# Single-buffered score banks and a fourth bank for the maxima, in the attention loop of a Mamba-2 and mixture-of-experts layer

## The reference, cut to what matters

```python
# b = 2, s = 2048, d = 256, 16 heads of 16
q, k, v = (src @ w).reshape(b, s, 16, 16).transpose(0, 2, 1, 3)   # for w in q_w, k_w, v_w
scores = einsum('bhqd,bhkd->bhqk', q, k) / sqrt(16)
scale = sigmoid(einsum('bhsd,hd->bhs', q, scale_w)) * 2.0
aw = softmax(scores * scale[..., None], axis=-1)
out = einsum('bhqk,bhkd->bhqd', aw, v)
```

## Time and profile before

| | us |
|---|---|
| runs: median (lowest to highest) | 2485.02 (2483.46 to 2487.04) |
| profiled execution: its span | 2487.7 |
| profiled execution: time outside its span | not given |
| TensorE busy | 2369.6 |
| VectorE busy | 2102.9 |
| ScalarE busy | 1796.4 |
| first to last maximum (L1682) | 720.5 to 2094.9 |
| first to last exponential (L1647) | 776.7 to 2137.4 |

### The profile page before, as it was taken

How to read it: one execution, slowest core, us unless ns; L and a number is a source line. 1 busy time by engine, 2 the same in 40 slices (tenths; PEclk the granted TensorE clock), 3 DMA queues, 4 the chain that set the end, 5 groups by cost and what they waited for, 6 DMA issues and landing times. The chain is left out here.

```text
span 2487.7 us, 45337 instructions
## 1 busy us (share of the span) xinstructions
PE 2369.6 (95%) x16331; PEld 1028.3 (41%) x16331; DVE 2102.9 (85%) x4156; ACT 1796.4 (72%) x2368; POOL 992.7 (40%) x1186
## 2 busy tenths in 40 slices
PE   7899999999689999999999999999999999996996
PEld 5566655655443223223222222223223222473663
DVE  6778788989689999999998999898899996283886
ACT  4888887777334887878787787787787878762664
POOL 1687878888741222211221221221211011255664
PEclk8999999999889999999999999999999999997998
DMA  3322233223240220304012030040040000125892
GB/s 110 112 88 90 85 92 105 89 99 96 67 137 14 37 43 7 59 14 65 14 31 35 14 59 7 14 65 2 14 65 2 2 2 24 52 83 204 297 304 101
DMA packets 105956, 174.09 MB, mean 70 GB/s; under 512 B 21218, under 2 KB 80658, under 8 KB 100596
## 3 DMA queue, kind: packets, MB, share of 16 engines
q1 hardware_dynamic: 98996, 156.08, 23.6%
q0 software_dynamic: 6016, 14.49, 1.7%
q10 hardware_dynamic: 720, 0.62, 0.1%
HBM read 145.21 MB, written 27.02 MB: 69 GB/s over the span
## 5 line engine op out<-in xcount | busy, mean ns | idle before, releaser
L1682 DVE TENSOR_REDUCE max_part<-round_psum 128x1 f32<-128x512 f32 x2048 | 1269.0, 683 | 101.8 <-PE round_psum L1591 96.8
L1647 ACT ACTIVATE p_exp<-score_psum 128x1024 f32<-128x1024 f32 x1024 | 993.3, 1022 | 213.7 <-PE score_psum L1576 209.3
L1591 PE MATMUL round_psum<-k_stack,q_stack 64*128 64x512 bf16 x2048 | 705.5, 384 | 10.7 <-DVE max_part L1682 6.5
L1567 PE MATMUL score_psum<-q_stack,k_stack 64*128 64x512 bf16 x2048 | 599.0, 379 | 0.9 <-ACT p_exp L1647 0.2
L1576 PE MATMUL score_psum<-q_stack,k_stack 35*128 35x512 bf16 x2048 | 594.6, 378 | 0.0
L1622 PE MATMUL pv_psum<-p_exp,values 128*17 128x512 f32 x4096 | 539.6, 598 | 0.0
L1591 PEld LDWEIGHTS round_psum<-k_stack,q_stack 64*128 64x128 bf16 x2048 | 189.4, 93 | 600.3 <-DVE max_part L1682 510.7
L672 PE MATMUL rot<-tokens_t,w_in 128*128 128x512 f32 x576 | 271.7, 603 | 0.2
L1576 PEld LDWEIGHTS score_psum<-q_stack,k_stack 35*128 35x128 bf16 x2048 | 188.9, 94 | 116.0 <-issue 0.5
L1729 POOL TENSOR_TENSOR rden<-pv_out,minus_one 128x16 f32<-128x16 f32 x31 | 90.0, 2903 | 332.4 <-ACT pv_out L1665 330.1
L1715 POOL CAST max_parts<-max_neg 128x16 bf16<-128x16 f32 x96 | 20.4, 212 | 365.8 <-DVE max_neg L1688 343.4
(11 more groups left out here) (300 smaller groups left out, 3472.9 us busy)
## 6 DMA issues: line engine op xcount, KB each, us to landing
cum_rows_in<-cum_rows SPq DMA_DIRECT2D x64, 512.0 KB, 3.8
expert_w<-in_expert_w SPq DMA_DIRECT2D x24, 1028.0 KB
tokens_t<-in_expert_w SPq DMA_DIRECT2D x15, 1028.0 KB
cum_pairs_in<-cum_rows SPq DMA_DIRECT2D x240, 64.0 KB, 2.8
qk_rows<-qk_parts SPq DMA_DIRECT2D x64, 192.0 KB, 3.1
q_stack<-qk_rows SPq DMA_DIRECT2D x84, 128.0 KB, 8.1
k_stack<-qk_rows SPq DMA_DIRECT2D x84, 128.0 KB, 9.1
token_rows<-tokens SPq DMA_DIRECT2D x12, 512.0 KB, 3.7
```

The source lines that it names most:

```text
L1567: nc.tensor.matmul(ebank[i // 2][:, i % 2, :], ks[rows, n % 2, plane, k * P:(k + 1) * P], qs[rows, n % 2, plane, q * BLK:(q + 1) * BLK], s ...
L1591: nc.tensor.matmul(bank[step][:, :], qs[rows, n % 2, plane, at:at + P], ks[rows, n % 2, plane, keys * BLK:(keys + 1) * BLK], start=True, s ...
L1647: nc.scalar.activation(pt[:, (k * 2 + pair) % 4, :, :], ebank[pair][:, :, :], ACT.Exp).then_inc(*exped.up(u, k, pair))
L1682: nc.vector.tensor_reduce(mx[:, c * HG + h, keys:keys + 1], bank[step][:, :], AX_X, ALU.max).then_inc(*maxed.up(u, k, i))
```

## The change

`round_psum` gets a fourth bank, and its users wait for the user four back. `score_psum` becomes three single banks. Scores take them in the order in which they begin (heads 1, 0, 3, 2 of each step), and each "main" waits until the exponential of the score three back has been taken. Each "rest" now raises `scored`, and ScalarE takes one head of 512 columns at a time. The stage before gets its fourth bank (half of `vbank`) from the ring, for which TensorE waits for that stage's last values (`first.v_stored`) ahead of its first maximum. The late values go around the three score banks.

```diff
-    ebank = [ps(f"score_psum{i}", [P, 2, BLK]) for i in range(2)]
+    ebank = [ps(f"score_psum{i}", [P, BLK]) for i in range(3)]
     pv = ps("pv_psum", [P, BLK])
-    rbank = [ps(f"round_psum{i}", [P, BLK]) for i in range(3)]
+    rbank = [ps(f"round_psum{i}", [P, BLK]) for i in range(4)]
...
-                                [ebank[0][:, i, :] for i in range(2)], [ebank[1][:, i, :] for i in range(2)], rbank[0:2])
+                                ebank[0:2], [ebank[2], rbank[3]], rbank[0:2])
...
-    bank = {u: rbank[i % 3] for i, u in enumerate(users)}
-    before = {u: users[i - 3] for i, u in enumerate(users) if i >= 3}
-
+    bank = {u: rbank[i % 4] for i, u in enumerate(users)}
+    before = {u: users[i - 4] for i, u in enumerate(users) if i >= 4}
+
+    scores = [(u, k, i) for u in range(NU) for k in range(KT) for i in (1, 0, 3, 2)]
+    score_bank = {score: ebank[i % 3] for i, score in enumerate(scores)}
+    score_before = {score: scores[i - 3] for i, score in enumerate(scores) if i >= 3}
...
-    scored = sems.events("scored", pairs)
-    exped = sems.events("exp_ready", pairs)
+    scored = sems.events("scored", scores)
+    exped = sems.events("exp_ready", scores)
...
-        return ebank[c // 2 % 2][:, c % 2, 0:D]
+        return ebank[c % 3][:, 0:D]
...
-                    stack_on_sync(nc, sp_, S, u, j, i, scored.at((u - 1) * SB - 1, KT - 1, 1) if u >= 2 else None)
-
-            sp_.wait_ge(*scored.at(NU - SB - 1, KT - 1, 1))
+                    stack_on_sync(nc, sp_, S, u, j, i, scored.at((u - 1) * SB - 1, KT - 1, 2) if u >= 2 else None)
+
+            sp_.wait_ge(*scored.at(NU - SB - 1, KT - 1, 2))
...
+            pe.wait_ge(*first.v_stored)
             for step in order:
...
-                    if i % 2 and (u, k) != (0, 0):
-                        pe.wait_ge(*exped.at(*back(u, k, 1), i // 2))
+                    if (u, k, i) in score_before:
+                        pe.wait_ge(*exped.at(*score_before[u, k, i]))
...
-                    nc.tensor.matmul(ebank[i // 2][:, i % 2, :], ks[rows, n % 2, plane, k * P:(k + 1) * P],
+                    nc.tensor.matmul(score_bank[u, k, i][:, :], ks[rows, n % 2, plane, k * P:(k + 1) * P],
...
-                    if i % 2 == 0:
-                        m.then_inc(*scored.up(u, k, i // 2))
+                    nc.tensor.matmul(score_bank[u, k, i][:, :], ks[rows, n % 2, plane, k * P:(k + 1) * P],
+                                     qs[rows, n % 2, plane, q * BLK:(q + 1) * BLK], start=False,
+                                     stop=True).then_inc(*scored.up(u, k, i))
...
-                        pe.wait_ge(*first.v_stored)
-                    if c - 4 in late:
-                        pe.wait_ge(*v_stored.at(c - 4))
+                    if c - 3 in late:
+                        pe.wait_ge(*v_stored.at(c - 3))
...
-                            pe.wait_ge(*exped.at(u, k, h // 2))
+                            pe.wait_ge(*exped.at(u, k, h))
...
-                if what == "rest" and i % 2 == 0:
+                if what == "rest":
                     pair = i // 2
-                    act.wait_ge(*scored.at(u, k, pair))
-                    if (u, k) >= (0, 2):
+                    act.wait_ge(*scored.at(u, k, i))
+                    if i % 2 and (u, k) >= (0, 2):
                         act.wait_ge(*weighed.at(*back(u, k, 2), pair))
-                    nc.scalar.activation(pt[:, (k * 2 + pair) % 4, :, :], ebank[pair][:, :, :],
-                                         ACT.Exp).then_inc(*exped.up(u, k, pair))
+                    nc.scalar.activation(pt[:, (k * 2 + pair) % 4, i % 2, :], score_bank[u, k, i][:, :],
+                                         ACT.Exp).then_inc(*exped.up(u, k, i))
```

More of the change, by code:

```diff
@@ L1575, in _ @@
                             pe.wait_ge(*S.filled.all())
-                    m = nc.tensor.matmul(ebank[i // 2][:, i % 2, :], ks[rows, n % 2, plane, k * P:(k + 1) * P],
-                                         qs[rows, n % 2, plane, q * BLK:(q + 1) * BLK], start=False, stop=True)
-                    if i % 2 == 0:
-                        m.then_inc(*scored.up(u, k, i // 2))
+                    nc.tensor.matmul(score_bank[u, k, i][:, :], ks[rows, n % 2, plane, k * P:(k + 1) * P],
+                                     qs[rows, n % 2, plane, q * BLK:(q + 1) * BLK], start=False,
+                                     stop=True).then_inc(*scored.up(u, k, i))
                 if what == "max":
```

## The result

The changed kernel takes 2664.65 us (median of four runs, 2660.55 to 2665.32), the kernel before 2485.06 on the same chip: a ratio of 1.072, 95% interval 1.0704 to 1.0735, 180 us more. The forecast was 2668.

A forecast was written before the change was run, and what follows sets the result against it. VectorE's maxima (2.48 a step) were taken as the bound, nearly tied with TensorE. A same-step wait makes 511 periods of 2.83: 1446 + 24 + 71 = 1541, +182, with entry +184; span 2671, forecast 2668, range 2635 to 2702.

The forecast's parts named there:

- Head 2's "main" behind head 1's exponential: Attention step: head 2's first score matmul waits for head 1's exponential of the same step until 1.31; period 2.83, not 2.47.
- Sum over the attention: Attention loop: 511 periods of 2.83 (1446), 24 for turns and 71 for group insertions: 1541 us in place of 1359.8.
- ScalarE is not the bound: Attention step: four 512-column exponentials occupy ScalarE for 2.0 to 2.1 us against 1.94, which by throughput still fits into 2.47.
- Entry: Before the first maximum: TensorE waits for all value copies of the stage before, 1.8 us later, straight on the path.
- Total: Whole kernel: +184 us makes the profiled span 2671; less 2.7 for span against median, the forecast is 2668.
- Who set the step before: Old attention step: VectorE's four maxima at 0.620 fill the 2.48 period, nearly tied with TensorE's 2.39 to 2.40.
- rival A: Attention loop: same-step wait covered, fourth maxima bank saves up to 0.62 at each of 39 insertions, 24 us, 2461; chance 4%.
- The ring of four: Maxima's banks: removes the 0.08 wait at the sixth matmul pair, already counted, and gives nothing more in a plain step.
- Clock: Attention loop: TensorE keeps granted clock 1.00 despite longer pauses; the rival of a lost fast clock, 2790, had chance 5%.

## Why the prediction was right, and where it was not

- **Head 2's "main" behind head 1's exponential.** Right in each link: 0.65, 0.60, then "main" at 1.30 (1.31 forecast), the value matmuls at 1.84 (1.85), the period 2.82 to 2.83 (2.83), and 2.81 in the last unit, where 2.83 was forecast. The halved exponentials show that this chain carries the step, and that ScalarE's load does not.
- **Sum over the attention.** 1537.3 measured, 1541 forecast; the plain step of 2.82 and not 2.83 makes up the difference. An output's turn adds 0.59 (forecast 0.58), the rows' turn 0.21 (0.21), a projection 1.92 (1.92), a pair of casts 0.26 (0.27), a scale 1.01 (1.07).
- **ScalarE is not the bound.** Right: four exponentials in 2.17, 0.65 idle. The 2.17 holds a hidden pause: head 3's exponential starts 0.59 behind head 0's, as it waits for its "rest". Where nothing waits, four take 2.06 (the run with four score banks), within the forecast 2.0 to 2.1, and start 0.48 apart, not 0.50 to 0.52. Splitting alone costs 6 us, or nothing where the scores have four banks.
- **Entry.** TensorE waited 1.98 for the last values' copies (forecast 1.8), but the row of the first maximum, 719.4 against 720.5, does not show it:

```profile
718.73 1.04 PE L1594 MATMUL round_psum<-k_stack,q_stack 64*128 64x512 bf16 x4 [1.98 <-ACT values L1292]
```

  The stages before ended a few us earlier in this execution; over the kernels here the first maximum lies between 712.4 and 720.5, so such a term can't be read from one trace. The 20 steps ahead of the scores, which I had at nothing, gave back 3.6 (55.9 to 52.3, against the changed kernel with a ring of three).
- **Total.** 2664.65 against 2668, but not every part was as close. The span is 2662.4, where the sum gave 2671: 4 less in the loop, 7 less ahead of it (5.0 shorter, not 1.8 longer), 2.2 more behind it. That the forecast took off another 2.7, for the distance of one execution from the median, brought it nearer by luck: here the median stands 2.3 above the profiled span.
- **Who set the step before.** Wrong. I divided VectorE's busy time by its count, got 0.62 and took that for its pace; its pace is 0.598. TensorE's wait of 0.08 at the sixth pair, which I had seen, was the ring's chain. This didn't harm the sum, because the new step was built from TensorE's pieces alone. It does show in VectorE's idle time, which is 0.42 a step (2.82 less four times 0.60) and not 0.35: the hidden pause comes on top. It did harm rival A: had the fourth bank been free, it would by my estimate have been worth 0.08 on each of 491 steps, some 39 us and not 24. The run with maximum 0 halved, 35 us, fits that size.
- **The ring of four.** "Nothing more in a plain step" was right; I had allowed it a share at insertions, and it has none.
- **Clock.** At 1.00 through the changed kernel's loop, as forecast (the stretch's row: length, PE, PEld, DVE, ACT, POOL busy, clock, DMA share, GB/s):

```profile
772.00:2312.00 1540.00, 1396.58 (x10558) 327.15 (x10556) 1230.06 (x2000) 1205.06 (x2234) 257.12 (x403) 1.00 0.14 24
```

## What to carry to other kernels

For a ring of n banks, write down for each user which earlier user frees its bank, and look for pairs inside one step: there the latency of the whole path (matmul, hand-over, other engine, hand-over) counts, not any engine's throughput. With this rotation over three score banks the period is that latency (1.30) plus the longest stretch without a new score (1.52), and moving the stretch only moves the wait. Shortening it (bfloat16 values) shortens the period by as much, to 2.18, with the wait still there; a fourth bank removes the wait. A busy time over a count is an engine's pace only where it is never late; compare it with a stretch where it certainly runs back to back.

## What the runs showed of the hardware

- A 512-column exponential out of PSUM takes 0.597 us; four in a row with nothing to wait for take 2.06 and start 0.48 apart. 256 columns less save 0.21.
- Two VectorE reductions of 0.68 in a row start 0.598 apart, so pauses of up to 0.08 between them leave no idle time in the rows.
- The granted clock stood at 0.50 through a stretch of 48 us, in which TensorE counted as busy for 44: at 1.2 GHz the same matmuls last longer (0.60 against 0.39) and look like load. The clock row, not the busy share, shows it.
